# Gated cross-attention and a ternary feed-forward layer: the attention's projections taken from single precision to 16-bit halves, and a new order of steps on all five engines

## What is computed

```python
def xattn(x, context, Wq, Wk, Wv, Wo):          # 16 heads of 16
    q, k, v = heads(x @ Wq), heads(context @ Wk), heads(context @ Wv)
    attn = softmax(q @ k.T * 16 ** -0.5)
    return merge(attn @ v) @ Wo

def ffn(x, W1, b1, W2, b2):                     # 256 -> 1024 -> 256
    h = gelu(x @ ternary(W1).T + b1)
    return h @ ternary(W2).T + b2

x = x + tanh(g_xattn) * xattn(layernorm(x), ctx, Wq, Wk, Wv, Wo)
x = x + tanh(g_ffn) * ffn(layernorm(x), W1, b1, W2, b2)
```

## Time and profile before

| | |
|---|---|
| time, median of 3 runs | 1662.82 us (1661.55 to 1668.23) |
| the profiled execution's own time | 1664.17 us |
| its span in the profile | 1662.4 us |
| mean granted TensorE clock, as a share of full speed | 0.984 |
| busy share of the span: PE, DVE, ACT, POOL | 91%, 90%, 57%, 40% |
| DMA | 117.93 MB in 207471 packets, 71 GB/s |
| the chain that ended last, by engine | PE 55%, DVE 26%, "issue" 13%, ACT 3% |

### The profile page before, as it was taken

The page is one execution under the profiler, slowest core; times in us unless marked ns, Lnnn a source line. Parts: engine busy times, 40 slices in busy tenths (PEclk is TensorE's granted clock), DMA queues, the critical chain, the costliest instruction groups (busy, mean ns, idle before and its releaser), DMA issues.

```text
span 1662.4 us, 48262 instructions
## 1 busy us (share of the span) xinstructions
PE 1508.0 (91%) x14501; PEld 1007.7 (61%) x14501; DVE 1489.1 (90%) x4379; ACT 939.8 (57%) x1799; POOL 668.8 (40%) x813
## 2 busy tenths in 40 slices
PE   3899999999999999999999999987999999999998
PEld 2566666666666666666666666655666666666665
DVE  7799999999999999999999999987888888888886
ACT  2456666665656666565656566654555555555554
POOL 5354555455555545554555545552111111111111
PEclk9899999999999999999999999996999999999999
DMA  2333333333333333333333333321010110101101
GB/s 78 92 99 85 96 84 88 93 86 97 84 96 83 97 84 94 86 87 95 86 97 83 98 83 95 81 49 55 26 38 25 38 38 25 38 25 38 38 25 51
DMA packets 207471, 117.93 MB, mean 71 GB/s; under 512 B 24912, under 2 KB 207184, under 8 KB 207440
## 3 DMA queue, kind: packets, MB, share of 16 engines
q1 hardware_dynamic: 207440, 117.54, 26.2%
HBM read 32.53 MB, written 16.78 MB: 30 GB/s over the span
## 4 chain that ended last, share of the span: by engine, by line
PE 55%; DVE 26%; issue 13%; ACT 3%; DVEq 2%; ACTq 0%; DMA 0%
PE bank L1069 12%; PE bank L312 9%; PE bank L1098 5%; PE bank L1099 5%; DVE smax L751 5%; PE bank L336 5%; PE bank L319 4%; PE bank L303 4%; DVE rstd L691 3%; DVE xres L796 3%; DVE k L721 3%; PE bank L392 2%; DVE rstd L693 2%; DVE y L1056 2%; DVE rstd L684 2%
## 5 line engine op out<-in xcount | busy, mean ns | idle before, releaser
L924 POOL TENSOR_TENSOR probl<-prob 128x512 f16<-128x512 f32 x512 | 529.2, 1042 | 531.2 <-ACT prob L602 530.3
L602 ACT ACTIVATE prob<-bank,masks 128x512 f32<-128x512 f32 x512 | 345.4, 688 | 138.9 <-PE bank L371 138.9
L751 DVE TENSOR_REDUCE smax<-bank 128x4 f32<-128x512 f32 x512 | 348.2, 681 | 13.5 <-PE bank L336 9.7
L1085 DVE TENSOR_TENSOR hidl<-hid 128x512 f16<-128x512 f32 x256 | 226.0, 883 | 80.5 <-ACT hid L1080 79.7
L1080 ACT ACTIVATE hid<-bank,b_sb 128x512 f32<-128x512 f32 x256 | 176.1, 688 | 211.3 <-PE bank L1069 205.3
L1069 PE MATMUL bank<-y,w1T 128*128 128x512 f16 x1024 | 264.6, 381 | 29.2 <-DVE y L1056 28.0
L1163 POOL TENSOR_TENSOR xres<-xres,b2g 128x1024 f32 (+1 forms) x32 | 75.7, 2366 | 431.4 <-ACT yln L1033 413.5
L1098 PE MATMUL bank<-w2T,hid 128*128 128x256 f16 x1024 | 237.4, 273 | 0.6 <-ACT w2T L1013 0.6
L1099 PE MATMUL bank<-w2T,hidl 128*128 128x256 f16 x1024 | 237.4, 273 | 0.0
L336 PE MATMUL bank<-k_rows,q_rows 64*128 64x128 f16 x2048 | 226.8, 220 | 5.6 <-DMA q_rows<-smaxT 3.4
L371 PE MATMUL bank<-q_rows,k_rows 64*128 64x128 f16 x2048 | 201.7, 219 | 0.8 <-DMA q_rows<-smaxT 0.8
(11 more groups left out here) (92 smaller groups left out, 2555.7 us busy)
## 6 DMA issues: line engine op xcount, KB each, us to landing
q_rows<-q SPq DMA_DIRECT2D x512, 64.0 KB, 2.5
k_rows<-k SPq DMA_DIRECT2D x512, 64.0 KB, 2.5
xres<-in_x_dram SPq DMA_DIRECT2D x64, 256.0 KB, 2.7
out_dram<-ystage SPq DMA_DIRECT2D x32, 512.0 KB, 2.9
ctx_sb<-in_ctx_dram SPq DMA_DIRECT2D x64, 192.0 KB, 3.2
q_rows<-smaxT SPq DMA_DIRECT2D x128, 8.0 KB
w_raw<-in_L_ffn_W_dram SPq DMA_DIRECT2D x2, 1024.0 KB, 7.0
prob<-in_L_xattn_Wq_dram SPq DMA_DIRECT2D x1, 256.0 KB, 4.2
```

Of the source, the lines that this page charges most:

```text
L602: act.activation(prob[u][:], st_bank[u % 2][:], ACT.Exp, bias=0.0, scale=masks[g.parity][:, 2 + b:3 + b]).then_inc(exp_done, 1)
L751: dve.tensor_reduce(smax[:, b, u * UH:(u + 1) * UH], sm_bank[u % 2][:].rearrange("p (h j) -> p h j", h=UH), AX.X, ALU.max).then_inc(max_ta ...
L924: pool.tensor_tensor(probl[u][:], prob[u][:], prob[u][:].bitcast(BF16)[:, 1::2], ALU.subtract).then_inc(prob_split, 1)
```

## The change

**Halves in place of single precision.** x, the context and the weighed values are split into two 16-bit parts before (x, context) or after (weighed values) their transposes; the weights are split once at the start, multiplied by 64. POOL makes x's and the context's lower parts in place (`low_x`, `low_ctx`): a single-precision number's upper 16 bits stay where they are, and the remainder is written over its lower 16. `transpose_x` then transposes both parts, eight transposes of 16 bits, and one ACT copy takes all of them to SBUF. Each projection runs three products per piece (`SPLIT`): high by high, high by low, low by high. For the weighed values ACT copies the high part (`copy_attnT`) and DVE makes the low one (`low_attn`). `low_prob` writes in place too, and `probl` is gone.

```diff
+        def halves(x, part):
+            return x.bitcast(F16)[:, (1, 0)[part]::2]
...
+                for k in range(KD):
+                    for b in range(2):
+                        o = ((part * KD + k) * 2 + b) * S
+                        last = pe.transpose(tr_bank[:].bitcast(F16)[:, o:o + S],
+                                            halves(xln[:, b, k * P:(k + 1) * P], part), ident16[:])
             last.then_inc(x_transposed, 1)
             return [(xT_copied, g.n + 1)]
...
+        SPLIT = ((0, 0), (0, 1), (1, 0))
+        def by_batch(m):
+            return pj_bank[:].rearrange("p (b m s) -> p m b s", m=KD, b=2)[:, m]
+        def typed(x, part):
+            return x.bitcast((BF16, F16)[part])
...
         def project_q(pe, g, m):
             if m == 0:
                 pe.wait_ge(xT_copied, g.n + 1)
             for k in range(KD):
-                last = pe.matmul(pj_bank[:, m * T:(m + 1) * T], wq_sb[:, k, m * P:(m + 1) * P],
-                                 xlnT[:, k, :], start=(k == 0), stop=(k == KD - 1))
+                for i, (wp, xp) in enumerate(SPLIT):
+                    last = pe.matmul(by_batch(m), wq16[:, wp, k, m * P:(m + 1) * P],
+                                     typed(xT16[:, xp, k, :], xp).rearrange("p (b s) -> p b s", b=2),
+                                     start=(k == 0 and i == 0 and m == 0), stop=(k == KD - 1 and i == 2),
+                                     skip_group_check=True)
             if m == KD - 1:
...
-            pe.wait_ge(attnT_copied, n + 1)
+            pe.wait_ge(attnT_split, n + 1)
             for k in range(KD):
-                last = pe.matmul(tr_bank[:, 0:D], attnT[:, k, :], wo_sb[:, k, :], start=(k == 0),
-                                 stop=(k == KD - 1))
+                for i, (wp, xp) in enumerate(SPLIT):
+                    last = pe.matmul(tr_bank[:, 0:D], attnT16[:, xp, k, :], wo16[:, wp, k, :],
+                                     start=(k == 0 and i == 0), stop=(k == KD - 1 and i == 2))
             last.then_inc(projected, 1)
...
                 act.wait_ge(q_made, g.n)
-            act.copy(xlnT[:].rearrange("p k t -> p (k t)"), tr_bank[:]).then_inc(xT_copied, 1)
+            act.copy(xT16[:].rearrange("p i k t -> p (i k t)"), tr_bank[:].bitcast(F16)).then_inc(xT_copied, 1)
...
+        def low_x(pool, g):
+            pool.wait_ge(ln_done, 2 * (g.n + 1))
+            x = xln[:].rearrange("p b d -> p (b d)")
+            pool.tensor_tensor(x.bitcast(F16)[:, 0::2], x, x.bitcast(BF16)[:, 1::2], ALU.subtract).then_inc(x_split, 1)
+        def low_ctx(pool, g):
+            pool.wait_ge(ctx_loaded[g.parity], 16 * (g.half + 1))
+            x = ctx_sb[g.parity][:].rearrange("p b c -> p (b c)")
+            pool.tensor_tensor(x.bitcast(F16)[:, 0::2], x, x.bitcast(BF16)[:, 1::2], ALU.subtract).then_inc(ctx_split, 1)
+        def low_attn(dve, n):
+            dve.wait_ge(attnT_high, n + 1)
+            dve.tensor_tensor(attnT16[:, 1].rearrange("p k t -> p (k t)"), tr_bank[:, 0:KD * S],
+                              attnT16[:, 0].rearrange("p k t -> p (k t)"), ALU.subtract).then_inc(attnT_split, 1)
...
         def low_prob(pool, g, b, u):
             n = g.batch(b) * UNITS + u
             pool.wait_ge(exp_done, n + 1)
-            pool.tensor_tensor(probl[u][:], prob[u][:], prob[u][:].bitcast(BF16)[:, 1::2],
+            pool.tensor_tensor(prob[u][:].bitcast(F16)[:, 0::2], prob[u][:], prob[u][:].bitcast(BF16)[:, 1::2],
                                ALU.subtract).then_inc(prob_split, 1)
```

```diff
         def low_q(dve, g):
             dve.wait_ge(q_high, g.n + 1)
-            for b in range(2):
-                last = dve.tensor_tensor(q16[g.parity][:, 1, b], by_batch(pj_bank)[:, b], q16[g.parity][:, 0, b],
-                                         ALU.subtract)
-            last.then_inc(q_split, 1)
+            dve.scalar_tensor_tensor(q16[g.parity][:, 1].rearrange("p b m s -> p (b m s)"), pj_bank[:], 1.0 / WS,
+                                     q16[g.parity][:, 0].rearrange("p b m s -> p (b m s)"), ALU.mult,
+                                     ALU.subtract).then_inc(q_split, 1)
...
-                              ALU.add).then_inc(norm_read, 1)
+            dve.tensor_reduce(sums_of(half), pv[:, :, 0:2 * HD].rearrange("p h (two d) -> p h d two", two=2), AX.X,
+                              ALU.add).then_inc(sums_taken, 1)
...
-            dve.wait_ge(norm_read, n * 2 + (half + 1))
-            dve.tensor_tensor(attn[b][:, heads, :], attn[b][:, heads, :],
...
+            dve.tensor_tensor(attn[b][:, heads, :], sums_of(half),
                               rsum[:, b, heads].unsqueeze(2).to_broadcast([P, HB, HD]),
                               ALU.mult).then_inc(norm_done, 1)
...
+                    act.wait_ge(k_moved[b], 16 * MOVES * (g.n - 1))
+            act.activation(k16[g.parity][:, 0].rearrange("p b m s -> p (b m s)"), pj_bank[:], ACT.Identity, bias=0.0,
+                           scale=1.0 / WS).then_inc(k_high, 1)
```

```diff
                 for u in range(UNITS):
                     low_prob(pool, g, b, u)
-                    if b == 1 and u == 0 and left >= 1:
+                    k = b * UNITS + u
+                    if g.parity == 1 and left >= 6 and k >= 4:
+                        for i in range(2 * k - 8, 2 * k - 6):
+                            root_x(pool, g.half + 3, i)
+                    if g.parity == 0 and left >= 4 and k < 3:
+                        for i in range(2 * k + 8, 2 * k + 10):
+                            root_x(pool, g.half + 2, i)
+                    if k == 3 and left >= 3:
+                        low_x(pool, g.after(3))
+                    if k == 4 and left >= 1:
                         pick_masks(pool, g.after(1))
+                    if k == 6 and left >= 3:
+                        low_ctx(pool, g.after(3))
...
+                    norm_y(dve, Group(0, 0), (i,))
+                if g.parity == 1 and left >= 6 and i < SEED_PARTS:
+                    seed_x(dve, g.half + 3, i)
...
+            if left >= 4:
+                apply_x(act, g4)
```

**Order.** The rough scores come seven units ahead in place of six, and the steps around them are in another order on every engine. In `pe_group`, one turn:

```diff
+            scores(pe, g, 0, 0, (g, 1, 3))
             if not first:
                 weigh(pe, before, 1, 2)
-                tr = project_out(pe, g.batch(0) - 2, tr)
...
+            if left >= 2:
+                pe.wait_ge(v_split, g.n + 1)
+                project_q(pe, g2, 0)
...
+            scores(pe, g, 0, 1, (g1, 0, 0) if left >= 1 else None)
             if not first:
                 weigh(pe, before, 1, 3)
+            tr = transpose_max(pe, g, 1, tr)
...
+                project_q(pe, g2, 1)
                 tr = transpose_ctx(pe, g2, tr)
...
+            scores(pe, g, 0, 2, (g1, 0, 1) if left >= 1 else None)
             weigh(pe, g, 0, 0)
...
-            scores(pe, g, 0, 3, (g1, 0, 1) if left >= 1 else None)
+            if not first:
+                tr = project_out(pe, g.batch(0) - 2, tr)
...
+            scores(pe, g, 0, 3, (g1, 0, 2) if left >= 1 else None)
             weigh(pe, g, 0, 1)
...
-            scores(pe, g, 1, 0, (g1, 0, 2) if left >= 1 else None)
+            scores(pe, g, 1, 0, (g1, 0, 3) if left >= 1 else None)
...
+                tr = transpose_attn(pe, g.batch(0) - 1, 1, tr)
...
+            scores(pe, g, 1, 1, (g1, 1, 0) if left >= 1 else None)
...
+            if left >= 1:
+                if left >= 2:
+                    pe.wait_ge(k_split, g.n + 3)
+                project_v(pe, g1, 0)
             if left >= 3:
                 tr = transpose_x(pe, g.after(3), tr)
-            scores(pe, g, 1, 2, (g1, 1, 0) if left >= 1 else None)
...
+                tr = project_out(pe, g.batch(0) - 1, tr)
+            scores(pe, g, 1, 3, (g1, 1, 2) if left >= 1 else None)
```

512 lines of the change are left out of this document (307 added, 205 removed).

## The result

The change makes the kernel slower by a little: 1674.88 us median (1672.79 to 1675.77, 4 runs) against 1664.18 us of the kernel before on the same chip (1661.55 to 1668.23, 4 runs), ratio 1.006 with the 95% interval 1.0036 to 1.0085. Forecast was 1639, and faster. The profiled execution took 1672.79 us, its span is 1670.6.

What follows compares the result with a forecast made beforehand. DVE, partly locked out by POOL, was taken to set the 16.95 us turn. The new turn, mean 16.3 plus 0.25 of locks, is 16.55: over 62 turns 25 us less, 1 more at start and end, 1639 us, range 1600 to 1653.

Steps and rivals of the forecast that it cites:

- the length of the walk: One new turn followed handoff by handoff from the start of low_attn through the transpose and projection banks: 15.58 us without seeds.
- To the end of K's projection: First stretch of the turn, from low_attn through Q, output projection and scores to K's twelve matmuls: 5.88 us.
- To the second low_attn: Next stretch, K's high half, low half, then take_max, round and low on DVE: reached at 8.21 us.
- the lock that I booked apart: Waits of round_max and low_max on DVE for POOL, added to the turn: 0.25 us, between 0 and 1.5.
- To low_v: Third stretch, second low_attn, x's transposes and copy, maxima, V's projection and high halves: reached at 12.41 us.
- Home: Last stretch, low_v, add, transposes of the weighed values, scores, take_max to low_max: ends at 15.58 us.
- The turn with seeds: Turns with four bn_stats between round and low on DVE: 17.1 us, giving a mean of 16.3.
- x by four batches ... cover, at nothing: Loading x for four batches at once was counted as cover for transfers, at no gain or cost.
- Work sets the turn: Rival: DVE's 13.3 us of work with a lock or two sets the pace, 14.2 to 15.5 us, 1495 to 1575; chance 0.16.
- The locks come back: Rival: round and low on DVE wait for POOL at both places, 16.9 to 17.1 us, 1655 to 1671; chance 0.15.
- Three passes are no cheaper: Rival: mixed 16-bit projection matmuls on PE take 0.2 us each, 2.7 more on the path, near 1800; chance 0.06.
- The clock falls: Rival: PE stands still for much over 1 us every turn, its clock halves, 17.5 to 18.6 us, 1700 to 1765; chance 0.25.

Runs made afterwards that it cites:

- norm_only: Kernel before with only the layer norm taken from the change, single precision and old order kept: 1619.10 us, ratio 0.9728.
- spare_idle: Changed kernel with one spare DVE memset a turn in front of low_v, where DVE stands idle: 1673.02 us, ratio 1.0049 to the kernel before.
- spare_chain: Changed kernel with the spare DVE memset a turn ahead of batch 0's low_attn, on the chain of handoffs: 1731.74 us, ratio 1.0409 to the kernel before.
- v_early: Changed kernel with V's second projection and its high and low halves moved ahead of x's transposes: 1678.91 us, ratio 1.0081 to the kernel before.
- bn_spread: Changed kernel with four bn_stats singly in the even turn, small seed parts moved in the odd turn, x loaded a turn sooner: 1670.36 us, ratio 1.0022 to the kernel before.
- v_max: Changed kernel with V's second half and batch 0's maxima both moved ahead of x's transposes: 1620.45 us, ratio 0.9731 to the kernel before.
- v_max_bn2: Changed kernel with V's second half and maxima ahead of x's transposes, bn_stats singly in the even turn, x loaded a turn sooner: 1571.00 us, 0.9437 of the kernel before.

## Why the prediction was wrong

**Right: what bounded the kernel before.** DVE with its waits for POOL (norm_only: 16.95 to 15.67 and 16.78 us). **Right: what bounds it now**, the order through two banks (spare_idle and spare_chain), and the prices in it: projection matmuls 0.11 us apart, ACT's copies 1.01 and 1.00, low_v 0.80, DVE's idle 2.0 ahead of it against 1.9. DVE's work is 13.4 us a turn as forecast (626.06 of 800 us). The transposes in 16 bits are right too: eight hold PE 0.62 us (632.27 below), the last of them 0.22, so 0.057 each against 0.056. The rule that I weighed there (the Trainium skill, "TensorE: Matmul & The Clock Gate", section "Back-to-back issue gap", some 81 ns) did not hold in this trace.

**Wrong: the length of the walk**, 15.58 us home. The same turn in the trace goes from low_attn at 623.15 to low_attn at 639.62, 16.47: its terms were taken too small, most of all the step from the transposes of the weighed values to the scores, 0.26 for 0.72. PE's timeline, then ACT's, then DVE's (in brackets, how long the engine stood before and for whom):

```profile
619.62 0.43 PE L444 MATMUL bank<-ident,attn 128*128 128x128 f32 x2 [1.17 <-DVE xres L943]
619.98 0.23 PE L378 MATMUL bank<-k_rows,q_rows 64*128 64x128 f16 x1
...
623.70 0.22 PE L392 MATMUL bank<-ident,smax 128*32 128x128 f16 x1 [1.72 <-DVE attnT L838]
623.86 0.83 PE L337 MATMUL bank<-xT,wq 128*128 128x256 bf16 x6
...
626.40 0.83 PE L455 MATMUL bank<-wo,attnT 128*128 128x256 f16 x6 [0.64 <-ACT ctxT L601]
627.17 0.23 PE L378 MATMUL bank<-k_rows,q_rows 64*128 64x128 f16 x1
...
632.27 0.62 PE L306 MATMUL bank<-ident,xln 128*128 128x128 f16 x8 [0.84 <-DVE attnT L838]
...
634.16 0.83 PE L359 MATMUL bank<-wv,ctxT 96*128 96x256 f16 x6
...
637.44 0.43 PE L444 MATMUL bank<-ident,attn 128*128 128x128 f32 x2 [1.16 <-DVE xres L943]
638.16 0.22 PE L378 MATMUL bank<-k_rows,q_rows 64*128 64x128 f16 x1 [0.28 <-DVE smax L894]
```
```profile
624.86 0.60 ACT L610 ACTIVATE q<-bank 128x512 f16<-128x512 f32 x1 [0.64 <-PE bank L337]
...
635.16 0.85 ACT L629 ACTIVATE v<-bank,masks 128x256 f16<-128x256 f32 x2 [0.50 <-PE bank L359]
```
```profile
631.17 0.41 DVE L902 TENSOR_SCALAR smax<-smax 128x16 f16<-128x16 f32 x1
```

- *To the end of K's projection* 6.04 for 5.88: Q reaches ACT 1.00 us after its first matmul where I had 0.82 + 0.03, and the output projection holds PE 0.77, not 0.65.
- *To the second low_attn* 0.19 more: round_max, 0.41 for 0.17. This is the lock that I booked apart, 0.25 a turn; the measured mean is 0.282 - 0.174 for round_max, twice a turn, 0.22, and 0.04 each for low_max, 0.30 together:

```profile
L902 DVE TENSOR_SCALAR smax<-smax 128x16 f16<-128x16 f32 x94 | 26.5, 282 | 3.2
...
L909 DVE SCALAR_TENSOR_TENSOR smax<-smax 128x16 f16<-128x16 f32 x94 | 20.2, 215 | 2.4
```

- *To low_v* 4.33 for 4.20: V's way to ACT, 1.00 again.
- *Home* 3.58 for 3.17: from the transposes of the weighed values to the scores 0.72, not 0.26. The timeline puts 0.28 of it down to the maximum that DVE ends at 637.91. But in the odd turn the same scores start at 619.98, before that maximum ends (620.09), so they don't need it, and the step takes 0.36. The chain of waits calls 0.24 of it issue, time without a wait that the profile shows (below). It stands at the head of PE's loop of two turns, in every second turn; that the jump costs it is inferred.

```profile
637.92 0.24 issue
```

The turn with seeds took 17.72 where the walk gives 17.1 and the lock. There the step "x by four batches ... cover, at nothing" failed too: SP issues x's load behind the maxima, and the chain that ended last holds its 3.77 us up to the bn_stats at 621.75, 0.43 later than DVE was ready:

```profile
617.81 3.77 DMA xres<-in_x_dram
```

Over all such turns that wait is small (13 of 24 turns, 4.1 us), and the four bn_stats are the larger piece. But it and V's branch are of like length: with V out of the way it held v_early's odd turns.

All the larger misses went the same way. The mean turn is 17.10 us and not 16.55: 0.55 us a turn, 33 us in sixty turns, more than the 25 that I forecast to win. A hand walk counts the steps that it knows; none of my rivals said "the chain is longer than walked", and the forecast's own range left 0.6 us a turn below it but only 0.2 above.

**The rivals.** *Work sets the turn* fell with spare_idle. *The locks come back* near the size that was booked, 0.30 for 0.25. *Three passes are no cheaper* fell with the matmuls 0.11 apart. *The clock falls* did not decide here, but it is near, and it is what took the gains of v_early and bn_spread. My condition for it, that PE stands for much over 1 us, doesn't tell the cases apart. From 200 to 1000 us the changed kernel has 24 stands of 1.66 to 1.72 us ahead of the maxima, and the clock is 1.00 in the four us behind each. v_max has 23 of 1.65 or 1.66, of which 11 were followed by a fall, and v_early's stands of 2.65 us and more were followed by one in all but three. What decides, and whether transposes count as work of PE, no run showed.

**What the change lost.** Of its parts the layer norm alone gives 2.7%; with all of them PE's busy time goes from 740.87 us of 800 (shown above, at norm_only) to 609.84:

```profile
200.00:1000.00 800.00, 609.84 (x9260) 445.58 (x9258) 626.06 (x1782) 507.01 (x937) 558.90 (x982) 1.00 0.35 90
```

That is from 15.7 us a turn to 13.0, not to the 12 of the forecast. The order hands what PE gained to waits. That order repaired in two places, V and the maxima ahead of x, with the seeds in idle time and x loaded a turn sooner, is v_max_bn2.

## What to carry to other kernels

When work is taken from the bounding engine, look for the longest chain of handoffs next, and give a walked chain a margin upward: each step that is forgotten makes it longer. Test it with one spare instruction, once where the engine idles and once on the chain. Move parts of a change one by one: here one part alone was faster than the whole. And when a move gives nothing, look at the turns one by one before it is dropped: V's move won 1.04 us in every even turn, and a transfer and the clock took it back in the odd ones.

## What was not expected

- A shorter path can cost time through the clock: v_early's even turns won 1.04 us and its odd ones lost 1.00, 0.9 of it to the clock, and twelve more matmuls where PE stood made it 23 us faster.
- DVE instructions of 0.16 us on 128x4 elements took 0.91 and 1.01 beside POOL's products, with one input in SBUF beside a constant; in the changed kernel's places the same ones took 0.15 to 0.16. The Trainium skill, "SBUF — State Buffer", section "SBUF: two separate sides", says that a DVE instruction in a two-port mode, or with two inputs in SBUF, waits for a whole GpSimd instruction; the trace agrees about the wait. In which mode these instructions ran, no run shows.
- Q's and V's projections reach ACT 0.17 us behind their rows' end, K's 0.03 (629.19 to 629.22). Why is open.
